# Segment sums of a Mamba scan taken as differences of running sums, in a fused Mamba and mixture-of-experts block

## The chip, the cores and the metric

The kernel runs on one core of a Trainium2 chip. The metric is the device time of one launch in microseconds (us). Engines are named as in the profile: PE is TensorE, PEld its weight loads, DVE is VectorE, ACT is ScalarE, POOL is GpSimd, SP issues the DMAs.

## The reference, cut to what matters

Eight sequences of 512 tokens with 128 channels go through two branches, which are multiplied: a Mamba-2 layer with an MLP, and a gated causal attention (16 heads of 8) followed by four dense experts.

```
zxbcdt = x @ in_proj_w.T
dt = softplus(zxbcdt[..., -4:] + dt_bias)           # 4 heads
A = -exp(A_log)
h = h * exp(dt_t * A) + (dt_t * x_t) outer B_t      # scan over 512 tokens
y = h @ C_t
...
s = x1 + mlp(layernorm(x1)),  x1 = xn + out_proj(rms(y * silu(z)))
g = silu(x2 + moe(rms(x2))),  x2 = xn + attention(rms(xn))
out = x + s * g
```

The scan is computed in four chunks of 128 tokens. Inside a chunk, output t takes input s with the weight exp(sum of dt*A over the tokens s+1 to t), for s <= t and for each of four heads. These sums, a 128 x 512 block per chunk (source token by head and target token), are the segment sums that the change is about.

## The kernel before, in words

One instruction stream per engine is written out by hand, with semaphores (`wait_ge`) between them. The engines go through rounds. Round r runs `stage_b` (the tail of sequence r: projections, experts, MLP; interleaved with the head of sequence r+1: input projections, convolution, attention score maxima) and then `stage_a` (attention and scan of sequence r+1). There is one head-only start (r = -1), a loop of seven full rounds, and one tail-only end. So `stage_a` runs eight times.

`stage_a` has 24 score units e, six (u = 0 to 5) for each of four head groups g. The scan's chunk g is dealt with in the same group. For the order around the change:

- PE: `exp_scores_of_four` (two units at once, from u = 0, 2, 4) waits for both exponentials of the pair before (`p_sb`). Behind it, at u = 0, come `weigh_values(e-2)`, `turn_y(g-1)` (transposes of the gated output), and `segments(g)`; at u = 2 `weigh_values`, `turn_values(g-1)`, `scan_inputs(g)`; at u = 4 `weigh_values`, `scan_outputs(g)`, and `new_state(g)` or, in the last group, `prep_a` (transposes of the next sequence's input).
- ACT: `exponentiate(e)` for each unit; between them `evac_values(g-1)` behind e = 6g, `evac_y(g-1)` behind e = 6g+1, and the exponential of the segment sums (into `es`) at u = 3 (u = 2 in group 0).
- POOL: the causal select of each unit (L1723, `pm_sb`), which `weigh_values` waits for; `xw` for the state; `decays(r, c)`, which multiplies a triangle of ones by dt*A of a chunk for four heads into `rs` (L1707); and small steps of the next input norm (`first_norms`, at e = 11, 13, 17).
- DVE: score maxima, `scan_products`, `scan_weights`, `scan_combine` (three operations behind `scan_outputs`), `scan_state` (the state update that frees PSUM bank R[1] for the next `segments`), the final gate and join.

Segment sums before: `segments(c)` is one fp32 matmul of `after` (ones where s > t) by `rs`, 128 x 512, into R[1]. The profile shows one fp32 matmul as two MATMUL records.

At the end of a round PE does `turn_y(3)`, `weigh_values(22)`, and then in `stage_b` the output projection `op` (L706), the transposes of the last attention values (L713), and the qkv projection of the next sequence. ACT does `evac_y(3)`, `square_y(3)`, `evac_values(3)`.

`cumulate` forms the running sums of dt*A (16 columns), the sums behind each token, and the totals, from which ACT takes `dec` (L1125).

Of the kernel before, what the change touches and what calls it, by code (L numbers as in the profile page):

```python
# [30 lines left out]
F32R = mybir.dt.float32r  # L31
# [13 lines left out]
G = 4  # L45
# [48 lines left out]
def build(nc, x, weights, vectors, rows, consts, out):  # L94
    with ExitStack() as ctx:
# [83 lines left out]
        rs = sb("rs", [P, 2, NH, P])  # L179
        es = sb("es", [P, 2, NH, P])  # L180
        gm = sb("gm", [P, 2, P])
# [30 lines left out]
        h2a = rs[:].rearrange("p k h t -> p k (h t)")  # L212
        h2b = es[:].rearrange("p k h t -> p k (h t)")
        h1a = wm[:].rearrange("p k h t -> p k (h t)")
        h1 = sb("h1", [P, 2, L])
        h3a = sb("h3a", [P, L])
# [56 lines left out]
        cum_ps = signal("cum_ps", 1)  # L273
        seg_ps = signal("seg_ps", T)
# [31 lines left out]
        dec_sb = signal("dec_sb", 1)  # L306
        seg_sb = signal("seg_sb", T)
# [29 lines left out]
        sv_sb = signal("sv_sb", 1)  # L337
        moe_sb = signal("moe_sb", T * E)
# [19 lines left out]
        rs_sb = signal("rs_sb", T)  # L358
# [84 lines left out]
        def _(pe):  # L443
# [253 lines left out]
            def stage_b(r, tail, head):  # L697
# [3 lines left out]
                if tail:  # L701

                    pe.wait_ge(yT_sb, at(yT_sb, r, 0))
# [5 lines left out]

                    pe.wait_ge(oT_sb, at(oT_sb, r, 0))  # L710
                    pe.wait_ge(yz_sb, at(yz_sb, r, 0))
                    for t in range(T):
                        i = pe.transpose(R[3][:, t * P:(t + 1) * P], oT[:, 1, t * P:(t + 1) * P], ident)  # L713
                    i.then_inc(ot3_ps, 1)
# [127 lines left out]
                if head:  # L842
                    exp_scores(r, 0)
# [12 lines left out]
            def stage_a(r):  # L856
                scan_inputs(r, 0)
                for e in range(G * UNITS):
# [34 lines left out]
                weigh_values(r, G * UNITS - 2)  # L893
# [7 lines left out]
            pe.wait_ge(pool_set, 10)  # L901
            pe.wait_ge(dve_set, 7)
# [14 lines left out]
        def _(act):  # L917
# [201 lines left out]
            def stage_a(r, tail):  # L1119
# [37 lines left out]
            act.wait_ge(pool_set, 3)  # L1157
            act.preload_act_table_set(EXP_LN)
# [17 lines left out]
        def _(dve):  # L1176
# [145 lines left out]
            def stage_b(r, tail, head):  # L1322
# [91 lines left out]
                if tail:  # L1414
                    for n in range(2):
# [7 lines left out]
                       ALU.add).then_inc(sv_sb, 1)  # L1423
                for t in range(T):
# [11 lines left out]
                    if head and t < 2:  # L1436
                        maxima(r, MAX_AT[t])

# [114 lines left out]
            dve.tensor_copy(maskb[:], future).then_inc(dve_set, 1)  # L1553
            ts(wqk[:], row[:, R_QN:R_QN + HD].unsqueeze(1).broadcast_to([P, AH, HD]), HD ** -0.5, None,
               ALU.mult).then_inc(dve_set, 1)
            dve.wait_ge(dve_set, 3)
# [7 lines left out]
            dve.wait_ge(dve_set, 7)  # L1564
# [21 lines left out]
        def _(pool):  # L1586
# [79 lines left out]
            def time_steps(r):  # L1666
# [29 lines left out]
                pool.sem_inc(pool_passed, 1)  # L1696
                pool.wait_ge(rs_sb, at(rs_sb, r, 0))
# [3 lines left out]
            def decays(r, c, tail):  # L1701

                pool.wait_ge(dt_sb, at(dt_sb, r, DT_STEPS))
                if c == 0 and tail:
                    pool.wait_ge(up_ps, at(up_ps, r, 9))
                pool.wait_ge(seg_ps, at(seg_ps, r, c - 1))
# [123 lines left out]
```

## Time and profile before

| | us |
|---|---|
| median of 3 runs | 869.19 (869.1 to 870.39) |
| profiled execution | 868.79 |
| its span, first to last instruction | 867.1 |
| PE busy | 786.9 |
| DVE busy | 618.0 |
| ACT busy | 499.2 |
| POOL busy | 323.9 |
| mean granted clock of PE | 0.992 of full speed |

1.7 us of the execution's time lies outside the span. A busy share says how long an engine had work in it, not that it set the time: in most stretches two or three engines wait for one another in turn, and what counts is which wait ends last.

### The profile page before, as it was taken

How to read it: one execution, taken by the hardware profiler on the slowest of the kernel's cores; microseconds unless marked ns; L12 is line 12 of the kernel's file. 1: busy time of each engine (PE TensorE's matmuls, PEld its weight loads, DVE VectorE, ACT ScalarE, POOL GpSimd, SP SyncE). 2: the span in 40 equal slices, each digit the busy share in tenths (PEclk: the TensorE clock that was granted, in tenths of full speed). 3: DMA queues.
4: the chain of work that ended last, by engine and by line, in shares of the span. 5: the costliest groups of instructions: out<-in, count | busy, mean ns of one | idle time of the engine just before them, and what ended most of it. 6: DMA issues, size and time to landing. Idle time of an engine off the chain costs nothing. (4 is left out here: it accounts for less than half of the span.)

```text
span 867.1 us, 18101 instructions
## 1 busy us (share of the span) xinstructions
PE 786.9 (91%) x5472; PEld 481.4 (56%) x5472; DVE 618.0 (71%) x1469; ACT 499.2 (58%) x928; POOL 323.9 (37%) x600
## 2 busy tenths in 40 slices
PE   2779999998999989998999989999899998999897
PEld 1455554755556564654647555474556556474555
DVE  2776479775888768776696768877587876967634
ACT  2335784466754775457744667537765568446552
POOL 5424533153512717045340545227160362505400
PEclk9998999999999999999999999999999999999999
DMA  4000000000000000000000000000000000000000
GB/s 165 2 8 20 8 0 2 9 15 25 0 8 12 14 12 0 8 14 24 0 0 8 14 24 0 2 18 2 24 0 8 13 25 0 0 8 14 24 2 13
DMA packets 15145, 11.73 MB, mean 14 GB/s; under 512 B 1040, under 2 KB 13968, under 8 KB 14992
## 3 DMA queue, kind: packets, MB, share of 16 engines
q1 hardware_dynamic: 15120, 11.43, 4.4%
q8 instruction: 12, 0.20, 0.1%
q14 instruction: 13, 0.11, 0.0%
HBM read 7.76 MB, written 2.10 MB: 11 GB/s over the span
## 5 line engine op out<-in xcount | busy, mean ns | idle before, releaser
L1102 ACT ACTIVATE sb_pr<-S 128x768 f32<-128x768 f32 (+1 forms) x192 | 163.8, 879 | 135.6 <-PE S L445 135.6
L1199 DVE TENSOR_REDUCE sb_mx<-S 128x2 f32<-128x256 f32 (+3 forms) x256 | 197.7, 816 | 29.3 <-PE S L445 28.8
L1723 POOL TENSOR_SCALAR_AFFINE_SELECT sb_pr<-sb_pr 128x256 f32<-128x256 f32 (+1 forms) x192 | 99.4, 523 | 299.3 <-ACT sb_pr L1102 299.0
L445 PE MATMUL R<-sb_pr,sb_va 128*32 128x512 f32 (+3 forms) x1024 | 89.4, 444 | 9.7 <-POOL sb_pr L1723 7.6
L445 PE MATMUL R<-sb_W,sb_pr 128*128 128x96 f32 (+1 forms) x512 | 69.5, 276 | 0.0
L445 PE MATMUL R<-sb_xfT,sb_W 128*128 128x512 f32 x144 | 69.2, 602 | 0.0
L445 PE MATMUL S<-sb_kT,sb_qT 32*128 32x256 f32 (+3 forms) x512 | 56.3, 384 | 13.8 <-DVE sb_mx L1199 10.9
L1187 DVE RECIPROCAL sb_rden<-R 128x16 f32<-128x16 f32 x32 | 8.2, 258 | 83.9 <-PE R L563 53.4
L445 PEld LDWEIGHTS R<-sb_W,sb_pr 128*128 128x128 f32 x512 | 63.5, 192 | 3.8 <-issue 3.5
L445 PEld LDWEIGHTS S<-sb_kT,sb_qT 32*128 32x128 f32 x512 | 27.5, 183 | 66.4 <-DVE sb_mx L1199 58.7
L445 PE MATMUL S<-sb_qT,sb_kT 32*128 32x256 f32 (+3 forms) x512 | 56.3, 384 | 2.9 <-ACT sb_pr L1102 1.9
L445 PEld LDWEIGHTS S<-sb_qT,sb_kT 32*128 32x128 f32 x512 | 27.3, 183 | 53.5 <-ACT sb_pr L1102 33.6
L1433 DVE SCALAR_TENSOR_TENSOR sb_x<-R,sb_wts,sb_x 128x96 f32<-128x96 f32 x128 | 40.6, 317 | 22.8 <-PE R L445 19.5
L445 PE MATMUL S<-sb_maskb,sb_identb 128*128 128x128 bf16 (+1 forms) x384 | 49.4, 241 | 0.0
L445 PEld LDWEIGHTS R<-sb_pr,sb_va 128*32 128x32 f32 x1024 | 23.5, 108 | 34.9 <-POOL sb_pr L1723 20.2
L965 ACT ACTIVATE sb_pr<-R 128x512 f32<-128x512 f32 x32 | 19.1, 598 | 39.1 <-PE R L445 39.0
L445 PE MATMUL R<-sb_rs,sb_cst 128*128 128x512 f32 x64 | 35.8, 642 | 5.7 <-DVE sb_x L1433 2.9
L1707 POOL TENSOR_TENSOR sb_rs<-sb_cst,sb_dta 128x512 f32<-128x512 f32 x32 | 40.5, 1265 | 1.2 <-POOL sb_dta L1698 1.1
L1626 POOL TENSOR_TENSOR sb_qk<-sb_qk,sb_wqk 128x512 f32<-128x512 f32 x8 | 10.1, 1269 | 81.9 <-ACT sb_sq L1000 81.9
L450 PE MATMUL S<-sb_cst,sb_tokqk 128*128 128x128 f32 x256 | 32.7, 285 | 4.5 <-DVE sb_tokqk L1385 2.2
L445 PEld LDWEIGHTS S<-sb_maskb,sb_identb 128*128 128x128 bf16 x384 | 23.8, 97 | 21.2 <-issue 17.5
L1217 DVE SCALAR_TENSOR_TENSOR sb_cv<-sb_xc,sb_vec,sb_cv 128x512 f32<-128x512 f32 x48 | 35.2, 734 | 0.0
(217 smaller groups left out, 1709.0 us busy)
## 6 DMA issues: line engine op xcount, KB each, us to landing
sb_xin<-x SPq DMA_DIRECT2D x9, 256.0 KB, 2.9
sb_W<-weights SPq DMA_DIRECT2D x1, 2290.0 KB, 10.9
sb_qT<-sb_mT SPq DMA_DIRECT2D x128, 4.0 KB
sb_xres<-x SPq DMA_DIRECT2D x8, 256.0 KB, 2.8
out<-sb_xres SPq DMA_DIRECT2D x7, 256.0 KB, 2.3
sb_cT<-sb_xact SPq DMA_DIRECT2D x8, 128.0 KB, 2.3
sb_W<-weights SPq DMA_DIRECT2D x1, 514.0 KB, 5.8
sb_cst<-consts SPq DMA_DIRECT2D x1, 328.0 KB, 3.1
```

The costliest lines, as they stand in the source:

```text
L445: return pe.matmul(o, lhsT, rhs, start=start, stop=stop, skip_group_check=True)
L450: i = pe.transpose(o[:, t * P:(t + 1) * P], src(t), ident)
L965: act.activation(dst, R[k % 4][:, :], func, bias=bias).then_inc(act_up, 1)
L1102: act.activation(pr[:, e % 4, :, 0:n], S[pair_of_exp(e)][:, :, 0:n], ACT.Exp).then_inc(p_sb, 1)
L1187: dve.reciprocal(rden[:], view[:, :, :, HD]).then_inc(done, 1)
L1199: o = dve.tensor_reduce(mx[:, n // P - 1, g, heads[0]:heads[1] + 1], found[:, :, at_col:at_col + n], AX.X, ALU.max, negate=True)
L1217: stt(out=cv[:, n], in0=xc[:, n, k:k + L], scalar=vcol(V_CONVW + TAPS * n + k), in1=cv[:, n], op0=ALU.mult, op1=ALU.add).then_inc(conv_dve, 1)
L1433: stt(out=x2[:, t, MASKED:D], in0=R[(22 + t) % 4][:, e * OC:(e + 1) * OC], scalar=wts[:, t, e:e + 1], in1=x2[:, t, MASKED:D], op0=ALU.mult ...
L1626: tt(qk[:, :, 0].rearrange("p t h d -> p t (h d)"), qk[:, :, 0].rearrange("p t h d -> p t (h d)"), wqk[:].rearrange("p h d -> p (h d)").un ...
L1707: tt(rs[:, c % 2], upto.unsqueeze(1).broadcast_to([P, NH, P]), dta[:, c, :].unsqueeze(2).broadcast_to([P, NH, P]), ALU.mult).then_inc(rs_s ...
L1723: pool.affine_select(out=keep, in_=keep, compare_op=ALU.is_ge, fill=0.0, base=0, pattern=pattern, channel_multiplier=-1)\
```

## The change

The running sums of dt*A, which `cumulate` already leaves in PSUM, are taken as cs[t], and a segment sum is cs[t] - cs[s]. So that fp32r operands carry enough digits, each sum is split into a rounded part and the rest. `sums_in_parts` (DVE, two operations of 128 x 32 elements) writes the parts of all four chunks and heads, `turn_sums` (PE) turns them with one 128 x 128 transpose, ACT makes from it `seg_v` and four left operands `seg_l`, and POOL one right operand `seg_r`, once per round. `segments(c)` is then one fp32r matmul of `seg_l[c]` by `seg_r` and one bf16 matmul that adds the large negative mask. `decays` goes. ACT makes its five operands right behind `exponentiate(0)`. Moves: on ACT `evac_values(g-1)` goes behind e = 6g+1, and at the end ahead of `evac_y(3)`; on PE `weigh_values(22)` goes ahead of `turn_y(3)`, the L713 transposes ahead of `op`, and `prep_a` ahead of `scan_outputs(3)`. The hidden layer `h2a` gets a tensor of its own, and there are a few more operations in the set-up.

```diff
+            def turn_sums(r):
+                pe.wait_ge(cs_sb, at(cs_sb, r, 2))
+                pe.wait_ge(act_up, at(act_up, r, 17))
+                pe.transpose(R[1][:, 0:P], cs[:].rearrange("p c k -> p (c k)"), ident).then_inc(csT_ps, 1)
+
             def segments(r, c):
 
-                pe.wait_ge(rs_sb, at(rs_sb, r, c + 1))
+                pe.wait_ge(segl_sb, at(segl_sb, r, 1 + T))
+                pe.wait_ge(segr_sb, at(segr_sb, r, 1))
...
-                mm(R[1][:, :], after, rs[:, c % 2].rearrange("p h t -> p (h t)")).then_inc(seg_ps, 1)
+                mm(R[1][:, :], seg_l[:, c, :], seg_r[:].rearrange("p h t -> p (h t)"), True, False)
+                mm(R[1][:, :].rearrange("p (h t) -> p h t", h=NH), maskb[:],
+                   identb[:].unsqueeze(1).broadcast_to([P, NH, P]), False, True).then_inc(seg_ps, 1)
...
# PE, experts_down
+                if t == 3 and head:
+                    pe.wait_ge(segl_sb, at(segl_sb, r, 1 + T))
...
# PE, stage_b: the L713 transposes now stand ahead of op; behind experts_down(r, 0, head):
+                    turn_sums(r)
                     exp_scores(r, 0)
...
# PE, stage_a
-                        scan_outputs(r, g)
                         if g == T - 1:
                             prep_a(r)
-                        elif g > 0:
+                        scan_outputs(r, g)
+                        if 0 < g < T - 1:
                             new_state(r, g)
...
+                weigh_values(r, G * UNITS - 2)
                 turn_y(r, T - 1)
-                weigh_values(r, G * UNITS - 2)
...
# ACT, stage_a
                     exponentiate(r, e)
-                    if u == 0 and g > 0:
+                    if e == 0:
+                        act.wait_ge(csT_ps, at(csT_ps, r, 1))
+                        act.wait_ge(segr_sb, at(segr_sb, r, 0))
+                        act.activation(seg_v[:], R[1][:, 0:P], ACT.Identity, bias=seg_sums[:, 1:2],
+                                       scale=seg_sums[:, 0:1]).then_inc(segl_sb, 1)
+                        act.wait_ge(seg_ps, at(seg_ps, r, 0))
+                        for c in range(T):
+                            act.activation(seg_l[:, c, :], R[1][:, 0:P], ACT.Identity, bias=seg_low[:, c:c + 1],
+                                           scale=seg_high[:, c:c + 1]).then_inc(segl_sb, 1)
+                    if u == 1 and g > 0:
                         evac_values(r, g - 1)
-                    if u == 1 and g > 0:
                         evac_y(r, g - 1)
...
+                evac_values(r, G - 1)
                 evac_y(r, T - 1)
                 square_y(r, T - 1)
-                evac_values(r, G - 1)
...
# DVE, stage_b, ahead of the experts' sums
+                if head:
+                    sums_in_parts(r)
...
+            def sums_in_parts(r):
+
+                total = S[0][:, 0, 0:T * NH].rearrange("p (c h) -> p c h", h=NH).unsqueeze(2)\
+                    .broadcast_to([P, T, 2, NH])
+                parts = cs[:, :, 0:16].rearrange("p c (x y h) -> p c x y h", x=2, y=2)
+                dve.wait_ge(dec_sb, at(dec_sb, r, 1))
+                dve.wait_ge(csT_ps, at(csT_ps, r, 0))
+                dve.tensor_copy(parts[:, :, :, 0].bitcast(F32R), total).then_inc(cs_sb, 1)
+                dve.wait_ge(cs_sb, at(cs_sb, r, 1))
+                tt(parts[:, :, :, 1], total, parts[:, :, :, 0], ALU.subtract).then_inc(cs_sb, 1)
...
# POOL
-            def decays(r, c, tail):
...
             def stage_a(r, tail):
-                decays(r, 0, tail)
+                pool.wait_ge(segl_sb, at(segl_sb, r, 1))
+                pool.sem_inc(pool_passed, 1)
+                pool.wait_ge(seg_ps, at(seg_ps, r, 0))
+                tt(seg_r[:], seg_v[:].unsqueeze(1).broadcast_to([P, NH, P]),
+                   seg_head[:].unsqueeze(2).broadcast_to([P, NH, P]), ALU.mult).then_inc(segr_sb, 1)
...
-                    if u == 3 and g < T - 1:
-                        decays(r, g + 1, tail)
```

## Rows read from the trace of the kernel before

**Rows 1.** The page, part 1: busy time of PE.
```profile
PE 786.9 (91%) x5472; PEld 481.4 (56%) x5472; DVE 618.0 (71%) x1469; ACT 499.2 (58%) x928; POOL 323.9 (37%) x600
```

**Rows 2.** Timeline (start, length, instruction, idle): ACT, once a round.
```profile
260.46 0.21 ACT L1125 ACTIVATE sb_dec<-S 128x48 f32<-128x48 f32 x1 [3.27 <-PE S L445]
...
362.07 0.21 ACT L1125 ACTIVATE sb_dec<-S 128x48 f32<-128x48 f32 x1 [3.28 <-PE S L445]
...
465.01 0.21 ACT L1125 ACTIVATE sb_dec<-S 128x48 f32<-128x48 f32 x1 [3.27 <-PE S L445]
```

**Rows 3.** Timeline from 287.5 to 291.3: how group 2 begins.
```profile
287.59 0.51 PE L445 MATMUL S<-sb_qT,sb_kT 32*128 32x512 f32 x4
...
288.03 0.86 PE L445 MATMUL R<-sb_pr,sb_va 128*32 128x256 f32 x16
...
288.83 0.42 DVE L1511 TENSOR_TENSOR sb_hst<-R,sb_hdec 64x256 f32<-64x256 f32 x1
289.07 0.59 ACT L942 ACTIVATE sb_oT<-R 128x512 f32<-128x512 f32 x1
...
289.30 1.12 PE L445 MATMUL R<-sb_rs,sb_cst 128*128 128x512 f32 x2
...
289.55 1.03 ACT L1102 ACTIVATE sb_pr<-S 128x1024 f32<-128x1024 f32 x1
...
290.63 0.19 PEld L445 LDWEIGHTS S<-sb_qT,sb_kT 32*128 32x128 f32 x4 [1.03 <-ACT sb_pr L1102]
```

**Rows 4.** Groups by line and form, all engines: busy, mean ns of one.
```profile
L445 PE MATMUL S<-sb_maskb,sb_identb 128*128 128x256 bf16 x128 | 20.9, 276 | 0.0
L926 ACT ACTIVATE sb_va<-S,sb_ratio 128x128 f32<-128x128 f32 x32 | 11.5, 360 | 0.0
```

**Rows 5.** Timeline from 280 to 281.7: how group 1 begins.
```profile
280.12 1.02 PE L445 MATMUL R<-sb_rs,sb_cst 128*128 128x512 f32 x2
280.15 1.03 ACT L1102 ACTIVATE sb_pr<-S 128x1024 f32<-128x1024 f32 x1
...
281.23 0.19 PEld L445 LDWEIGHTS S<-sb_qT,sb_kT 32*128 32x128 f32 x4 [0.91 <-ACT sb_pr L1102]
```

**Rows 6.** Timeline from 294.5 to 301.7: how group 3 begins.
```profile
294.53 1.49 POOL L1707 TENSOR_TENSOR sb_rs<-sb_cst,sb_dta 128x512 f32<-128x512 f32 x1
...
295.04 1.52 DVE L1452 TENSOR_TENSOR sb_gs<-sb_x,sb_gs 128x512 f32<-128x512 f32 x1
...
298.15 0.86 PE L445 MATMUL R<-sb_pr,sb_va 128*32 128x256 f32 x16 [0.66 <-POOL sb_pr L1723]
...
299.69 1.12 PE L445 MATMUL R<-sb_rs,sb_cst 128*128 128x512 f32 x2 [0.31 <-DVE sb_hst L1511]
...
301.62 1.07 PE L445 MATMUL R<-sb_pr,sb_va 128*32 128x512 f32 x8 [0.42 <-POOL sb_pr L1723]
```

**Rows 7.** Timeline from 253 to 267.2: score masks; ACT and PE behind the first unit.
```profile
253.79 0.61 PE L445 MATMUL S<-sb_maskb,sb_identb 128*128 128x256 bf16 x4
...
262.67 1.02 ACT L1102 ACTIVATE sb_pr<-S 128x1024 f32<-128x1024 f32 x1 [2.00 <-PE S L445]
...
265.14 1.02 ACT L1102 ACTIVATE sb_pr<-S 128x1024 f32<-128x1024 f32 x1 [1.44 <-PE S L445]
...
267.18 0.61 PE L445 MATMUL R<-sb_W,sb_pr 128*128 128x96 f32 x4
```

**Rows 8.** Timeline from 306.6 to 312: the end of a round on PE.
```profile
308.33 0.44 PE L627 MATMUL R<-sb_cst,sb_yz 128*128 128x128 f32 x2 [0.99 <-DVE sb_yz L1499]
308.70 0.86 PE L445 MATMUL R<-sb_pr,sb_va 128*32 128x256 f32 x16
...
311.81 2.75 PE L445 MATMUL S<-sb_W,sb_xbT 128*128 128x384 f32 x8
```

**Rows 9.** Windows of 2 us from 426: busy by engine, then the granted clock.
```profile
428.00:430.00 2.00, 2.00 (x12) 2.00 (x11) 0.99 (x2) 1.15 (x4) 2.00 (x3) 0.50 0.00 0
```

**Rows 10.** Timeline: the last tail's value transposes on PE, and what waits.
```profile
822.00 0.66 PE L450 MATMUL R<-sb_cst,sb_ao 128*128 128x128 f32 x4 [0.68 <-DVE sb_ao L1189]
```

More of the change, by code:

```diff
@@ L178, in build @@
         dec = sb("dec", [P, 3, T, NH])
-        rs = sb("rs", [P, 2, NH, P])
         es = sb("es", [P, 2, NH, P])
+        cs = sb("cs", [P, T, 32])
+        seg_v = sb("seg_v", [P, P])
+        seg_l = sb("seg_l", [P, T, P], F32R)
+        seg_r = sb("seg_r", [P, NH, P], F32R)
+        seg_low = sb("seg_low", [P, T])
+        seg_high = sb("seg_high", [P, T])
+        seg_sums = sb("seg_sums", [P, 2])
+        seg_head = sb("seg_head", [P, NH])
         gm = sb("gm", [P, 2, P])
@@ L215, in build @@
         h1 = sb("h1", [P, 2, L])
+        h2a = sb("h2a", [P, 2, L])
         h3a = sb("h3a", [P, L])
@@ L273, in build @@
         cum_ps = signal("cum_ps", 1)
+        csT_ps = signal("csT_ps", 1)
         seg_ps = signal("seg_ps", T)
@@ L306, in build @@
         dec_sb = signal("dec_sb", 1)
+        segl_sb = signal("segl_sb", 1 + T)
         seg_sb = signal("seg_sb", T)
@@ L337, in build @@
         sv_sb = signal("sv_sb", 1)
+        cs_sb = signal("cs_sb", 2)
         moe_sb = signal("moe_sb", T * E)
@@ L701, in stage_b @@
                 if tail:
+                    pe.wait_ge(oT_sb, at(oT_sb, r, 0))
+                    pe.wait_ge(yz_sb, at(yz_sb, r, 0))
+                    for t in range(T):
+                        i = pe.transpose(R[3][:, t * P:(t + 1) * P], oT[:, 1, t * P:(t + 1) * P], ident)
+                    i.then_inc(ot3_ps, 1)
                     pe.wait_ge(yT_sb, at(yT_sb, r, 0))
@@ L708, in stage_b @@
                     i.then_inc(op_ps, 1)
[L710 to L714, printed above, removed]
                 if head:
@@ L900, in _ @@
             pe.wait_ge(c_loaded, 48)
-            pe.wait_ge(pool_set, 10)
-            pe.wait_ge(dve_set, 7)
+            pe.wait_ge(pool_set, 11)
+            pe.wait_ge(dve_set, 13)
             pe.wait_ge(xab_sb, at(xab_sb, -2, 1))
@@ L1157, in _ @@
             act.wait_ge(pool_set, 3)
+            act.wait_ge(dve_set, 6)
             act.preload_act_table_set(EXP_LN)
@@ L1553, in _ @@
             dve.tensor_copy(maskb[:], future).then_inc(dve_set, 1)
+            by_part = ident.rearrange("p (c k) -> p c k", c=T)
+            dve.tensor_reduce(seg_low[:], by_part[:, :, 0:8], AX.X, ALU.add).then_inc(dve_set, 1)
+            dve.tensor_reduce(seg_high[:], by_part[:, :, 8:16], AX.X, ALU.add, negate=True).then_inc(dve_set, 1)
+            dve.wait_ge(dve_set, 4)
+            dve.tensor_reduce(seg_sums[:, 0:1], seg_low[:], AX.X, ALU.add).then_inc(dve_set, 1)
+            dve.tensor_reduce(seg_sums[:, 1:2], seg_high[:], AX.X, ALU.add, negate=True).then_inc(dve_set, 1)
+            dve.tensor_reduce(sp[:, 0], by_part[:, :, 0:16].rearrange("p c (m h) -> p c h m", h=NH),
+                              AX.X, ALU.add).then_inc(dve_set, 1)
+            dve.wait_ge(dve_set, 7)
+            dve.tensor_reduce(seg_head[:], sp[:, 0].rearrange("p c h -> p h c"), AX.X,
+                              ALU.add).then_inc(dve_set, 1)
             ts(wqk[:], row[:, R_QN:R_QN + HD].unsqueeze(1).broadcast_to([P, AH, HD]), HD ** -0.5, None,
                ALU.mult).then_inc(dve_set, 1)
-            dve.wait_ge(dve_set, 3)
+            dve.wait_ge(dve_set, 9)
             tt(wqk[:], wqk[:], row[:, R_KN:R_KN + HD].unsqueeze(1).broadcast_to([P, AH, HD]),
@@ L1695, in time_steps @@
                 pool.wait_ge(cum_ps, at(cum_ps, r, 0))
-                pool.sem_inc(pool_passed, 1)
-                pool.wait_ge(rs_sb, at(rs_sb, r, 0))
                 tt(dta[:], dt[:], neg_a[:].unsqueeze(1).broadcast_to([P, T, NH]),
                    ALU.mult).then_inc(dt_sb, 1)
-            def decays(r, c, tail):
[L1703 to L1706, printed above, removed]
-                tt(rs[:, c % 2], upto.unsqueeze(1).broadcast_to([P, NH, P]),
-                   dta[:, c, :].unsqueeze(2).broadcast_to([P, NH, P]), ALU.mult).then_inc(rs_sb, 1)
-            def stage_a(r, tail):
-                decays(r, 0, tail)
+            def stage_a(r, tail):
+                pool.wait_ge(segl_sb, at(segl_sb, r, 1))
[3 more added lines that the diff above has]
+                   seg_head[:].unsqueeze(2).broadcast_to([P, NH, P]), ALU.mult).then_inc(segr_sb, 1)
                 for e in range(G * UNITS):
@@ L1748, in _ @@
             pool.memset(xc[:, :, 0:3], 0.0).then_inc(pool_set, 1)
+            pool.memset(cs[:], 0.0).then_inc(pool_set, 1)
             pool.memset(cT[:], 0.0).then_inc(pool_set, 1)
```

7 lines of the change are left out of this document (3 added, 4 removed).

## The prediction

> **What bounds the kernel now.** I read the page first. PE is busy for 91% of the span [rows 1], so it looks like the bound; but the change takes work from PE and POOL and gives some to ACT, and whether that pays is decided wait by wait. Next the round: ACT's `dec` comes at 260.46 and 362.07 [rows 2], so a full round lasts 101.61 us. `stage_a` runs eight times, and its rounds look alike.
>
> Then the timeline of one `stage_a`, around each `segments(g)`. In the middle of a group (u = 2 to 5) PE goes from one matmul into the next, and everything else is early. At its beginning it is not PE that decides. In group 2 the scores start at 287.59, the segment matmul runs from 289.30 to 290.42, and PE then waits: the next scores start at 290.63, behind ACT [rows 3]. ACT is held by `evac_values`, which stands between the two exponentials: it starts at 289.07, and the second exponential at 289.55. Group 1 is the same: segment matmul 280.12 to 281.14, scores at 281.23 [rows 5]. In group 3 two more waits appear: `weigh_values(16)` waits for POOL's select until 298.15, and `weigh_values(18)` until 301.62 [rows 6]. POOL had `decays(3)` from 294.53 to 296.02 ahead of these selects. The reader is to see three waits in these rows: ACT's order, POOL's queue, and the state update of DVE that lets each segment matmul begin.
>
> **The segment pass.** Out goes an fp32 matmul of 1.02 to 1.12 us [rows 3, 5]; in come an fp32r and a bf16 one of 512 columns. The trace has no fp32r matmul over 128 rows. The nearest row is the scores': four of 32 rows and 512 columns side by side in 0.51 us [rows 3], with the next instruction 0.44 behind their start. The bf16 mask of 256 columns takes 276 ns, and four of them 0.61 us [rows 4, 7], so each further one 0.11 and 512 columns 0.22. Together some 0.75 us until PE is free, 0.3 to 0.35 less than now. The bounds: half of that fp32r price, if the four row strips shared a rate that one matmul has alone (0.22 less), and the whole fp32 price (0.85 for the stream, so the pair is 0.2 slower than now). I take 0.44, since that is a measured spacing.
>
> The Trainium skill ("FP8 and Floating Point Precision", TensorE Precision Notes) says that true FP32 takes four passes through the array and reduced-precision FP32 is read and truncated; one of four passes of a 0.85 us stream would be 0.21 us, and the forecast some 2.5 us lower. The scores' 0.44 us [rows 3] doesn't show that price.
>
> **Group 1.** ACT now runs both exponentials in a row. The second would start 0.48 earlier (the 289.07 and 289.55 of [rows 3]), at 279.67, and end at 280.70 [rows 5]. The new segment pair frees PE at 280.12 + 0.75 = 280.87. So the scores go at 280.85 instead of 281.23: gain 0.38. What is late next is PE itself. `evac_values` and `evac_y` now come behind the exponential, in time the scores need anyway.
>
> **Group 2.** It starts 0.38 early. The state update of DVE ends at 289.25 before [rows 3], now 288.87; the segment pair frees PE at 289.67; the second exponential ends at 290.58 - 0.38 - 0.48 = 289.72. Scores at 289.77 against 290.63: 0.86 early in all, so 0.48 more. The select that `weigh_values` needs follows the exponential, thus moves with it.
>
> **Group 3.** It starts 0.86 early. The decays are gone from POOL, so selects 16 and 17 are done before PE asks, and the 0.66 wait [rows 6] goes. What is late next is the scan on DVE: the segment matmul waits for its state update (0.31 in the row) and starts at 299.69 [rows 6]. Ahead of it stands L1452, which took 1.52 us while POOL worked in the same time [rows 6]; without `decays` I give it 0.2 (the bounds: nothing and 0.6). So the segment pair starts 0.86 + 0.2 early, at 298.63, and is done at 299.45 (0.8 with its end) against 299.69 + 1.12 = 300.81: 1.35 early. Then `weigh_values(18)` no longer waits 0.42 [rows 6] for a select behind POOL's norm steps: 1.77 early.
>
> **Group 0.** The segment matmul gets shorter between waits for DVE's maxima; I cost it at nothing. Of the four shortened matmuls none pays by PE's work alone.
>
> **The end of the round.** `prep_a` (four transposes, 0.66 with their end [rows 10], so some 0.5 of PE) now stands ahead of `scan_outputs(3)`, and `weigh_values(22)` (0.86 [rows 8], 0.78 without its end) fills the wait for DVE, of which 0.99 is in the row of `turn_y(3)` [rows 8]. Moving 0.5 out of that hole and 0.78 into it, and a wait of 0.1 for `yT` behind the L713 transposes, leaves 0.2 gain, to the qkv projection at 311.81 [rows 8]. `prep_a` waits for DVE's norms and the last `seg_sb`; both are over 1 us early.
>
> **What is added.** `turn_sums` is one transpose, a quarter of four in 0.66 [rows 10], so some 0.15 us on PE, between `experts_down(0)` and the first scores; I count it in full. DVE's two small operations lie in its wait for the experts. The five ACT reads are the largest addition: 128 x 128 from PSUM takes 0.36 [rows 4], so 1.8 us behind the first exponential, 263.69 to 265.5. The second exponential stood at 265.14 [rows 7], so it comes 0.3 late, but PE asks for it only behind `experts_down(3)`. `experts_down(3)`, now waiting for `seg_l`, stands at 267.10 to 267.18 [rows 7]: 1.6 us of cover. At twice the price per read it would be gone, at 0.2 a round. POOL's one product (1.49 at most, as `decays` in [rows 6]) is queued ahead of the first select, whose result PE wants behind the experts and `segments(0)`, over 5 us later.
>
> **The sum.** Per round 0.38 + 0.48 + 0.91 + 0.2 - 0.15, = 1.82; eight times, 14.6 us. The head-only start loses some 1.15: there the sums, the transpose and ACT's reads have no experts to lie behind (0.7 and 0.3), and a memset is ahead of the first norm on POOL (0.15). The last tail gains 0.8: the value transposes come ahead of `op`, which covers the DVE step for which PE waited 0.68 [rows 10]. Net -14.3 on the profiled execution's 868.8 (867.1 span and 1.7 around it): 854.5. That execution is 0.4 below the median shown, so against the median 854.9.
>
> **The rivals.**
> - *Only POOL's queue pays.* ACT does the same work in another order, and if the next exponential is held by the displaced evacuations, the 0.38 and 0.48 are given back. For it: 0.59 of `evac_values` [rows 3] and the evacuation of y now stand together ahead of it. Against it: PE waits for the exponential before, not for this one. Left are 0.91 + 0.2 - 0.15 = 1 us a round: 861. The same time comes about when the fp32r pass costs like the fp32 one: then PE is free only 1.2 us behind each start, and groups 1 and 3 lose 0.4 each, some 862. Chance 0.17 together.
> - *Hidden anyway.* The shift made in `stage_a` is lost in `stage_b` to something that doesn't move with it, or the clock takes most of it: 867.5 to 871. Nothing in the rows is tied to a fixed time; the DMAs have microseconds of slack. Chance 0.04.
> - *Slower: the clock.* In one round, at 428 to 430, the granted clock stood at 0.50 [rows 9], the lower level of 1.2 GHz, after a sparse stretch of PE around the small projections, where it did not fall in the other rounds. That round took 102.94 us against 101.61 [rows 2]: one such dip costs 1.3 us. The change makes PE idler and shifts the rounds. One dip in every round would take back 6 x 1.3 = 8 us; from two in a round, 2.6 against the 1.8 gained, it decides: some 874. Against it: the waits that go are PE's, so busy share hardly falls. The Trainium skill ("TensorE: Matmul & The Clock Gate", What's actually happening) says that the throttled state is the default and activity releases it; by that rule an idler PE is at risk, and the row of the dip agrees with it. Chance 0.09.
> - *The forecast*, all three group starts pay: 0.70.
>
> **How the numbers follow.** Predicted 854.9. Cheap fp32r (-2.5), the 0.6 on L1452 (-2.8) and a cheaper end (-1.5) reach to 848; the first rival reaches to 862, and with a dip in some rounds 863. The range is 848 to 863; below it 0.08 is left and above it 0.12. Within 0.2% (1.7 us, about what a measurement can tell from no change): 0.04. Faster: 0.87. Slower: 0.09.
>
> **What the profile after would show.** Segment pairs of about 0.8 us. In groups 1 and 2, scores right behind the second exponential, about 0.4 and 0.9 us earlier in the round, `weigh_values(16)` without a wait for POOL, and 1.8 us gained by the qkv projection. POOL some 30 us less busy, ACT some 10 to 15 more. A round of 99.8 us. It would be wrong if ACT's reads took twice 0.36, if `experts_down(3)` or `prep_a` showed a wait, or if the clock were at 0.5 in stretches where it is now full.

## The result, and the profile after

| | before | after |
|---|---|---|
| median | 870.85 us (869.1 to 873.39, 20 runs) | 866.61 us (861.57 to 868.76, 20 runs) |
| ratio | | 0.9940, 95% interval 0.9925 to 0.9954 |
| profiled execution | 868.79 | 867.78 |
| its span | 867.1 | 865.9 |
| mean granted clock of PE | 0.992 | 0.973 |

The change gains 0.6%, 4 us; 854.9 was forecast, and the time lies outside the range of 848 to 863. The runs of after spread over 7.2 us where those of before spread over 4.3, and the time goes with the clock: the runs of 861.57 to 862.08 us show a mean of 0.983, those of 867.5 to 868.8 us 0.972 to 0.974.

The page, part 1 (busy time, share, instructions), of the kernel after, against [rows 1]:
```profile
PE 786.7 (91%) x5480; PEld 490.6 (57%) x5480; DVE 615.6 (71%) x1491; ACT 511.0 (59%) x968; POOL 296.0 (34%) x577
```
POOL lost 27.9 us and ACT gained 11.8, as expected. PE's busy time fell by 0.2 us only, although its work shrank: at a lower clock the same work is busy for longer, and the mean clock fell from 0.992 to 0.973. That is the first hint.

ACT's `dec` in the timeline of after, against [rows 2]:
```profile
262.46 0.21 ACT L1146 ACTIVATE sb_dec<-S 128x48 f32<-128x48 f32 x1 [3.28 <-PE S L455]
...
362.23 0.21 ACT L1146 ACTIVATE sb_dec<-S 128x48 f32<-128x48 f32 x1 [3.27 <-PE S L455]
...
464.79 0.21 ACT L1146 ACTIVATE sb_dec<-S 128x48 f32<-128x48 f32 x1 [3.28 <-PE S L455]
```
One round takes 99.77 us, 1.83 less than 101.60 and what was forecast (1.82). The next takes 102.56. The eight `dec` of an execution bound seven intervals: the first is the round behind the start, the other six are called the full rounds here:

| us | 1st (start) | full rounds 2 to 7 |
|---|---|---|
| before | 96.72 | 101.59, 101.61, 102.94, 101.60, 101.59, 101.60 |
| after | 97.83 | 101.23, 99.77, 102.56, 102.57, 102.60, 101.15 |

After has three lengths: 99.8, 101.2 and 102.6. In what follows a place is given by its distance behind the `dec` of its round, and a low stretch is one at a granted clock of 0.50. Windows of 2 us of after, 10 us behind the `dec` of 362.23 (PE, PEld, DVE, ACT and POOL busy, granted clock, DMA share, GB/s):
```profile
372.00:374.00 2.00, 1.10 (x5) 0.47 (x4) 1.93 (x6) 1.48 (x3) 0.99 (x2) 1.00 0.00 0
374.00:376.00 2.00, 1.96 (x12) 0.45 (x12) 1.85 (x4) 1.08 (x2) 0.41 (x1) 0.77 0.00 0
376.00:378.00 2.00, 2.00 (x18) 1.70 (x15) 0.81 (x2) 0.81 (x1) 0.17 (x1) 0.50 0.00 0
378.00:380.00 2.00, 2.00 (x21) 1.65 (x20) 1.37 (x6) 0.35 (x1) 0.47 (x1) 0.88 0.00 0
```
The same two windows of before:
```profile
372.00:374.00 2.00, 1.58 (x6) 0.60 (x6) 1.76 (x5) 1.08 (x3) 0.99 (x2) 1.00 0.00 0
374.00:376.00 2.00, 2.00 (x20) 0.87 (x20) 1.87 (x3) 1.36 (x4) 1.03 (x2) 1.00 0.00 0
```
In after PE's clock falls to its lower level, 1.2 GHz, behind a stretch in which PE was busy for 1.10 of 2 us; before it was busy for 1.58 there, and the clock held. Read over the whole trace, the full rounds of after hold eight such low stretches: five some 12 us behind `dec`, in group 0, of which one is shown, and three some 63 us behind it, around the small projections, where before had its only one [rows 9]. Rounds with none take 99.77, with one 101.15 or 101.23, with two 102.56 to 102.60: each costs 1.4 us. Six rounds took 609.88 us, and 6 x 99.77 would be 598.6: the low stretches cost 11.3 us of this execution. It took 867.78 us, 13.3 more than the 854.5 forecast for it.

A sparse place alone doesn't make the clock fall. This is the round of after that has no low stretch (262.46), and the disturbed one (362.23), each from 10 us behind its `dec`:
```profile
272.46:274.46 2.00, 1.25 (x6) 0.64 (x6) 1.93 (x6) 1.48 (x3) 0.99 (x2) 1.00 0.00 0
372.23:374.23 2.00, 1.26 (x6) 0.65 (x6) 1.93 (x6) 1.48 (x3) 0.99 (x2) 1.00 0.00 0
```
PE is as idle in the one as in the other, and the clock fell behind the second only. Before has 1.64 to 1.65 in these 2 us of every full round. So the change made the place sparser in all six rounds, and the clock fell there in five.

The timeline of PE in group 0 of before, same round:
```profile
372.29 1.10 PE L445 MATMUL R<-sb_rs,sb_cst 128*128 128x512 f32 x2 [0.41 <-DVE sb_x L1433]
373.32 0.44 PE L445 MATMUL S<-sb_qT,sb_kT 32*128 32x384 f32 x2
373.88 0.44 PE L445 MATMUL S<-sb_kT,sb_qT 32*128 32x384 f32 x2
```
and of after:
```profile
372.44 0.47 PE L455 MATMUL R<-sb_seg_r,sb_seg_l 128*128 128x512 f32 x1 [0.41 <-DVE sb_x L1465]
...
372.75 0.39 PE L455 MATMUL R<-sb_identb,sb_maskb 128*128 128x512 bf16 x1
...
373.07 0.44 PE L455 MATMUL S<-sb_qT,sb_kT 32*128 32x384 f32 x2
...
374.04 0.44 PE L455 MATMUL S<-sb_kT,sb_qT 32*128 32x384 f32 x2 [0.53 <-DVE sb_mx L1229]
```
Less `dec` (362.07 and 362.23), the second half of the scores goes at 11.81 in both. The shorter segment sum gained nothing up to there; it became 0.53 us of waiting for DVE, next to a wait of 0.41 that was there already. The prediction costed group 0 at nothing, nearly rightly as work. The wait that came of it is where the clock now falls.

The other place, around the small projections, is a different matter. PE in it, before (behind the `dec` of 260.46):
```profile
319.69 0.66 PE L450 MATMUL R<-sb_cst,sb_x1n 128*128 128x128 f32 x4 [0.92 <-DVE sb_x1n L1355]
...
321.97 0.66 PE L450 MATMUL R<-sb_cst,sb_xf 128*128 128x128 f32 x4 [0.32 <-DVE sb_xf L1369]
...
323.40 1.05 PE L445 MATMUL R<-sb_W,sb_xfT 128*128 128x4 f32 x8 [0.34 <-ACT sb_xfT L1032]
```
and after (262.46):
```profile
319.84 0.66 PE L460 MATMUL R<-sb_cst,sb_x1n 128*128 128x128 f32 x4 [0.93 <-DVE sb_x1n L1385]
...
322.12 0.66 PE L460 MATMUL R<-sb_cst,sb_xf 128*128 128x128 f32 x4 [0.33 <-DVE sb_xf L1399]
...
323.56 1.05 PE L455 MATMUL R<-sb_W,sb_xfT 128*128 128x4 f32 x8 [0.34 <-ACT sb_xfT L1053]
```
The waits are the same within 0.01 us. That this place has three low stretches where it had one is thus not because work was taken from it.

Groups 1 to 3 are nearly as foreseen. Group 2 in the undisturbed round, against [rows 3]:
```profile
289.58 1.94 ACT L1123 ACTIVATE sb_pr<-S 128x1024 f32<-128x1024 f32 x2 [1.86 <-PE S L455]
...
290.25 0.42 DVE L1554 TENSOR_TENSOR sb_hst<-R,sb_hdec 64x256 f32<-64x256 f32 x1
...
290.73 0.49 PE L455 MATMUL R<-sb_seg_r,sb_seg_l 128*128 128x512 f32 x1
...
291.06 0.10 PEld L455 LDWEIGHTS R<-sb_identb,sb_maskb 128*128 128x128 bf16 x1
291.06 0.39 PE L455 MATMUL R<-sb_identb,sb_maskb 128*128 128x512 bf16 x1
291.40 0.60 ACT L963 ACTIVATE sb_oT<-R 128x512 f32<-128x512 f32 x1
291.57 0.19 PEld L455 LDWEIGHTS S<-sb_qT,sb_kT 32*128 32x128 f32 x4 [0.41 <-ACT sb_pr L1123]
```
The next matmul goes 0.33 us behind the start of the fp32r pass. The two exponentials stand together (x2, from 289.58), and `evac_values` starts at 291.40, behind both. Scores go at 291.57, 29.11 behind `dec`; before at 30.17 (290.63 - 260.46).

Group 3, against [rows 6]:
```profile
295.99 1.12 DVE L1495 TENSOR_TENSOR sb_gs<-sb_x,sb_gs 128x512 f32<-128x512 f32 x1
...
297.57 2.07 POOL L1666 TENSOR_TENSOR sb_lnv<-sb_lnv,sb_minus_half 128x8 f32<-128x8 f32 x1
...
298.37 0.86 PE L455 MATMUL R<-sb_pr,sb_va 128*32 128x256 f32 x16
...
300.32 0.47 PE L455 MATMUL R<-sb_seg_r,sb_seg_l 128*128 128x512 f32 x1 [0.43 <-DVE sb_hst L1554]
...
302.02 1.07 PE L455 MATMUL R<-sb_pr,sb_va 128*32 128x512 f32 x8 [0.61 <-POOL sb_pr L1770]
```
`weigh_values(16)` (at 298.37) no longer waits. DVE's step (L1495, L1452 before) takes 1.12 where it took 1.52, the 0.4 within its bounds. But `weigh_values(18)` (at 302.02) still waits for POOL, 0.61, behind the norm steps (2.07 for one of them): the prediction's step that said this wait goes was wrong.

### The profile page after: what moved, and what is told of

It reads as the page before. It is cut to its first block and busy times, and to the rows that moved or that the text cites. A ratio compares the mean times of both kernels' runs of the same rounds, so it can differ in the third digit from the quotient of the medians.

```text
span 865.9 us, 18165 instructions
## 1 busy us (share of the span) xinstructions
PE 786.7 (91%) x5480; PEld 490.6 (57%) x5480; DVE 615.6 (71%) x1491; ACT 511.0 (59%) x968; POOL 296.0 (34%) x577
## 5 line engine op out<-in xcount | busy, mean ns | idle before, releaser
L1123 ACT ACTIVATE sb_pr<-S 128x768 f32<-128x768 f32 (+1 forms) x192 | 161.7, 883 | 127.0 <-PE S L455 127.0
L455 PE MATMUL R<-sb_pr,sb_va 128*32 128x512 f32 (+3 forms) x1024 | 93.4, 460 | 6.6 <-POOL sb_pr L1770 4.3
L455 PE MATMUL S<-sb_kT,sb_qT 32*128 32x256 f32 (+3 forms) x512 | 58.3, 393 | 17.0 <-DVE sb_mx L1229 14.7
L1757 POOL TENSOR_TENSOR sb_seg_r<-sb_seg_v,sb_seg_head 128x512 fp32r<-128x512 f32 x8 | 8.3, 1042 | 174.9 <-ACT sb_seg_v L1154 174.9
L455 PE MATMUL S<-sb_qT,sb_kT 32*128 32x256 f32 (+3 forms) x512 | 58.3, 393 | 1.7 <-ACT sb_pr L1123 0.8
L460 PE MATMUL S<-sb_cst,sb_tokqk 128*128 128x128 f32 x256 | 38.7, 321 | 3.5 <-DVE sb_tokqk L1415 2.2
L460 PEld LDWEIGHTS S<-sb_cst,sb_tokqk 128*128 128x128 f32 x256 | 36.1, 169 | 5.2 <-DVE sb_tokqk L1415 2.6
L1680 POOL TENSOR_TENSOR sb_qk<-sb_qk,sb_wqk 128x512 f32<-128x512 f32 x8 | 10.2, 1270 | 79.8 <-ACT sb_sq L1021 79.8
```

What stands on the lines that cost most here:

```text
L455: return pe.matmul(o, lhsT, rhs, start=start, stop=stop, skip_group_check=True)
L460: i = pe.transpose(o[:, t * P:(t + 1) * P], src(t), ident)
L1123: act.activation(pr[:, e % 4, :, 0:n], S[pair_of_exp(e)][:, :, 0:n], ACT.Exp).then_inc(p_sb, 1)
L1680: tt(qk[:, :, 0].rearrange("p t h d -> p t (h d)"), qk[:, :, 0].rearrange("p t h d -> p t (h d)"), wqk[:].rearrange("p h d -> p (h d)").un ...
L1757: tt(seg_r[:], seg_v[:].unsqueeze(1).broadcast_to([P, NH, P]), seg_head[:].unsqueeze(2).broadcast_to([P, NH, P]), ALU.mult).then_inc(segr_ ...
```

## The experiments

Three theories stood. **A**: work was taken from PE where it waits anyway, PE gets idler there, and its clock falls. **B**: the low stretches hang on the length of the round and on when its places come, not on the work in them. **C**: the added work costs more than was reckoned. A "filler" is the kernel's own `dense`: fp32 matmuls of 256 columns whose result nobody reads. Ratios are against the kernel before on the same chip, with 95% intervals. Counts of low stretches are of each kernel's one traced execution.

**Fillers in group 0 (e1), around the small projections (e2), in both (e3).** To the kernel after:
```diff
# e1, PE, stage_a, at e = 3, and ahead of segments(r, 0)
+    dense(R[3][:, 0:256], 1)
# e2, PE, stage_b: ahead of the transposes of x1n (2) and xf (1), and of the gate's matmuls (1)
+    if head:
+        dense(R[1][:, 0:256], 2)
```


> The changed kernel with two more fp32 matmuls of 256 columns per round on PE, whose results nobody reads, in the two waits of group 0: one between the masks of unit 2 and segments(0), one between exp_scores(3) and max_scores. Theory A (the work that the change takes away lets PE's clock fall): the stretches at a granted clock of 0.5 in group 0 of the full rounds (five in the profile of the changed kernel) go, those in stage_b stay, and the time falls by 5 to 7 us to about 860. Theory B (the clock falls by the round's length and phase, wherever PE stands): as many stretches as before, elsewhere, 866. Theory C (what is lost is the added work of ACT and PE, not the clock): 866 to 868, with the matmuls on top.

> The changed kernel with four more such matmuls per round in stage_b, in the waits ahead of the x1n transposes (two), the xf transposes (one) and the gate (one). Theory A: the stretches at 0.5 in stage_b (four in the profile of the changed kernel) go, those in group 0 stay; the time falls by 4 to 5 us to about 862. Theory B: no fewer stretches, 866 to 868. Theory C: 866 to 868.

> Both sets of added matmuls. Theory A: a full round takes 99.8 to 100.2 us every time, with no stretch at 0.5 in the seven full rounds; 854 to 857. Theory B: 865 or more. Theory C: 866 to 869.

Measured: e1 864.15 us (0.9909, 0.9883 to 0.9935), e2 858.97 (0.9865, 0.9849 to 0.9881), e3 859.07 (0.9855, 0.9836 to 0.9873). Theory A had said 860, 862 and 854 to 857: e2 is faster than that, e1 and e3 are slower, and e1's interval overlaps that of after (0.9925 to 0.9954). In the full rounds of e1 no low stretch was left at 12 us; behind the start, the tail included, there are four at 60 to 63 and three new ones at 39. Its traced execution, at 870.13 us, is the slowest of its six; it is at the lower clock for 17.1 us behind the first `dec`, and its second `dec` comes 3.1 later than that of after. In e2 those at 63 are gone from the full rounds, and two remain there at 12. In the full rounds of e3 two remain, both at 39. The place of the new ones, in windows of e1 (columns as above):
```profile
403.00:405.00 2.00, 1.50 (x8) 0.16 (x8) 0.52 (x2) 1.93 (x3) 1.26 (x4) 0.72 0.45 131
405.00:407.00 2.00, 2.00 (x13) 1.89 (x9) 0.55 (x2) 0.00 (x0) 0.01 (x1) 0.50 0.45 124
```
That is the part of group 3 in which PE waits for DVE's state update and POOL's select. Added work made the kernel faster in e2 and e3, which C can't give, and each place that was filled lost its low stretches in the full rounds, for A. But a place that was quiet in after took some over, and in e2 the clock fell at 12 in two rounds of six, although PE was as idle there as in after (1.24 to 1.26 us of 2) in all six: in which round, and at which of several sparse places, the clock falls is not fixed by the place alone, and so much of B stands.

**The moves alone (e4).** The kernel before, with the moves on ACT and PE and the old segment sums:
```diff
-                    if u == 0 and g > 0:
+                    if u == 1 and g > 0:
                         evac_values(r, g - 1)
...
-                turn_y(r, T - 1)
                 weigh_values(r, G * UNITS - 2)
+                turn_y(r, T - 1)
```


> The kernel before with the moves alone: evac_values behind the second exponential and ahead of evac_y(3), weigh_values(22) ahead of turn_y(3), the L713 transposes ahead of op, prep_a ahead of scan_outputs(3); segment sums as before, with decays on POOL. By my steps the moves give 0.2 in groups 1 and 2 (PE is then held by the 1.1 us segment matmul, not by ACT), nothing in group 3 (POOL's queue stays), 0.2 at the end and 0.8 in the last tail: 0.5 a round, 5 us, 865 to 866. If the moves alone carry the gain: 859 or less. If they give nothing without the shorter pass: 869 to 870. The clock should stay at full speed in group 0, as the fp32 matmul stands there.

Measured 860.09 us (0.9872, 0.9858 to 0.9887): 6.5 us faster than the whole change, and 5 faster than expected. Full rounds take 100.53 us, 1.07 less than before, none with a low stretch. The expectation gave 0.5 a round, since PE would be held by the long segment matmul. By the places of `weigh_values` behind `dec` the moves alone give 0.35 in group 1 and 0.47 in group 2, nearly all of the forecast's 0.38 and 0.48, nothing in group 3, and 0.25 at the end of the round. So these two steps need ACT's order only, not the shorter pass.

**The segment sums alone (e6).** The kernel after with every move undone.

> The changed kernel's segment sums alone: every move (the evacuations on ACT, the last weighing, the turned values and the turned input on PE) is undone. The moves alone gave 1.07 us a round against the kernel before and brought no low stretch in full rounds. Theory A: undisturbed rounds of 100.8 to 101.2 us (0.4 to 0.8 under the 101.60 of before), with low stretches at about 12 us behind dec, since the shorter passes of group 0 are here, perhaps at 64 too; then 868 to 873, no faster than the kernel before. Theory B (phase of the round): no fixed place. Theory C (the low stretches need the moves and the segment sums together): none in full rounds and 863 to 866.

Measured 870.95 us (1.0011, 0.9990 to 1.0033): no gain. Undisturbed rounds take 100.89, 0.71 less than before, which over six rounds is 4.3 us; but three of the six have a low stretch, two at 40 us and one at 12, at 1.4 to 1.6 us each. Of the 0.71, 0.14 comes in group 0 and 0.56 in group 3, nothing in groups 1 and 2. The two halves are worth 1.07 and 0.71 a round, 1.78 against the 1.83 together: they add up. Theory A gave the time and the round's length, but it had put the low stretches at 12.

**The first segment sum in full fp32 (e5).** The work in one place changes, and nothing is added whose result isn't used. To the kernel after:
```diff
-                mm(R[1][:, :], seg_l[:, c, :], seg_r[:].rearrange("p h t -> p (h t)"), True, False)
+                left, right = seg_l[:, c, :], seg_r[:].rearrange("p h t -> p (h t)")
+                if c == 0:
+                    left, right = left.bitcast(F32), right.bitcast(F32)
+                mm(R[1][:, :], left, right, True, False)
```


> The changed kernel, but the first of the four segment sums of a round is taken in full fp32 (the same operands, read as fp32); nothing else moves. The pass then takes about 1.0 us where it took 0.5, in group 0 alone, where PE waits for DVE anyway (0.41 and 0.53 us). Theory A (a PE whose work was taken away lets its clock fall): the low stretches some 12 us behind dec go, as they did when filling matmuls were put in that place; those 63 us behind dec in the small projections stay, perhaps with one at 39. Rounds without a low stretch 99.8 us, time 860 to 866. Theory B (the low stretches follow from the length and the phase of the round, not from the work in the place): as many low stretches as in the changed kernel, 866 to 868. Theory C (the full fp32 pass costs its own time): rounds without a low stretch 100.3 us.

Measured 859.45 us (0.9854, 0.9834 to 0.9875), 7 us faster than after, with one pass a round made slower. Timeline of PE in e5, 10 us behind its `dec` of 361.08:
```profile
371.30 1.10 PE L455 MATMUL R<-sb_seg_r,sb_seg_l 128*128 128x512 f32 x2 [0.42 <-DVE sb_x L1468]
372.23 0.38 PE L455 MATMUL R<-sb_identb,sb_maskb 128*128 128x512 bf16 x1
372.54 0.44 PE L455 MATMUL S<-sb_qT,sb_kT 32*128 32x384 f32 x2
372.90 0.44 PE L455 MATMUL S<-sb_kT,sb_qT 32*128 32x384 f32 x2
```
The second scores go at 11.82, as in after (11.81), now without a wait. PE is busy for 1.77 to 1.78 of the 2 us from 10 us behind `dec`. No low stretch stands at 12, and only one in all full rounds, at 39. The rounds without one take 100.08, 0.31 more than 99.77: C's price for it. That the low stretches at 63 went too, where nothing was changed, is more than A had said, and speaks for the part of B that stands.

**Every sparse place filled (e7).** The places of e1 and e2, two in group 3 and five fillers in the head-only start:
```diff
+                    if not tail:
+                        dense(R[0][:, 0:256], 2)
                     turn_sums(r)
                     exp_scores(r, 0)
...
+                        if g == 3:
+                            dense(R[3][:, 0:256], 1)
                         segments(r, g)
```


> The changed kernel with matmuls of 256 columns, whose results nobody reads, in every wait of PE near which a low stretch was seen: two in group 0, four around the small projections, two in group 3, and five in the head-only start. Theory A: no low stretch in the full rounds, each 99.8 us; the low stretch of 10 to 14 us in the start is shorter; 853 to 856, near the forecast of 854.9. Rival (the fillers cost what they cover, or the low stretches appear in another place, as the one at 39 us did when group 0 alone was filled): 858 to 861.

Measured 854.27 us (853.81 to 855.23; 0.9809, 0.9796 to 0.9823), the fastest of all kernels here and 0.6 from the forecast. The page, part 1, of e7:
```profile
PE 798.4 (94%) x5610; PEld 499.4 (59%) x5610; DVE 614.3 (72%) x1491; ACT 510.1 (60%) x968; POOL 297.0 (35%) x577
```
Timeline of PE in its group 0:
```profile
367.87 0.65 PE L455 MATMUL R<-sb_cst 128*128 128x256 f32 x2
368.45 0.47 PE L455 MATMUL R<-sb_seg_r,sb_seg_l 128*128 128x512 f32 x1
...
369.45 0.70 PE L455 MATMUL R<-sb_cst 128*128 128x256 f32 x2
370.08 0.44 PE L455 MATMUL S<-sb_kT,sb_qT 32*128 32x384 f32 x2
```
PE does 12 us more and the kernel ends 12 us sooner. Six full rounds take 99.74 to 99.80 us, the clock is at 0.999, and the one low stretch stands at the very end. The fillers lie in the waits and cost the round nothing (99.77 in the undisturbed round of after). Against after, the profiled spans differ by 13.8: 11.3 in the six rounds, 2.6 ahead of the second `dec`.

**Control: fillers where PE had no wait (e8).** To the kernel after, in group 1 at u = 4:
```diff
+                        if g == 1:
+                            pe.wait_ge(gm_sb, at(gm_sb, r, g + 1))
+                            dense(R[2][:, 0:256], 2)
```


> Control: the changed kernel with two such matmuls a round at a place where PE has no wait (group 1, ahead of the last part of the group). Theory A: the low stretches at 12 and 63 us behind dec stay as in the changed kernel, since nothing is filled there, and the rounds are up to 0.9 us longer: 867 to 874. Theory B (any change of the round's length shifts the low stretches away): fewer of them, 860 to 865.

Measured 876.00 us (1.0067, 1.0043 to 1.0092). This is 2 us above the range of A. The full rounds hold eight low stretches, five of them at 12, two at 42 and one at 66. A longer round with more work on PE doesn't help in itself, which speaks against B as the whole cause. The rounds' own cost was more than expected: the one without a low stretch took 101.33, 1.56 above 99.77, where up to 0.9 was said. Timeline of PE in that round:
```profile
183.72 1.13 PE L455 MATMUL R<-sb_cst 128*128 128x256 f32 x4 [0.47 <-DVE sb_gm L1519]
184.78 0.85 PE L455 MATMUL R<-sb_pr,sb_va 128*32 128x384 f32 x8
```
The two fillers take 1.06, and the `wait_ge` that was put ahead of them holds PE for 0.47 more. So the control adds a short wait as well as work; no low stretch stands near it (24 us).

Over the 14 traced kernels PE is busy for 1.24 to 1.26 us of the 2 from 10 us behind `dec` in four (after, e2, e6, e8), and in 13 of their 24 full rounds the clock fell there. In the other ten it is busy for 1.64 or more, and in their 60 full rounds the clock never fell there.

**The same fillers in the kernel before (e9).**

> The kernel before, with the same filling matmuls as in e7_fill_all. This tells what the fillers are worth without the change. Theory A (the kernel before loses to the clock only one low stretch in its full rounds and part of the start, where e7 lost nothing more): full rounds stay at 101.60 us, without the one of 102.94; the start gains about 1 to 2 us; 866 to 868, ratio 0.995 to 0.998. Then the change itself, with the clock held in both, is worth 12 to 14 us. Rival (most of the 17 us that e7 gained over the kernel before come from the fillers, not from the change): 858 to 862.

Measured 873.12 us (1.0032, 1.0022 to 1.0043), worse than before. Both expectations had it faster than before. All full rounds take 102.00 to 102.03, without a low stretch, 0.4 more than 101.60. The second scores of group 0 go 12.25 us behind `dec`, 0.42 later than in before, and that is all that the round loses: before has no wait as long as the filler there (0.63 us). The first `dec` comes 3.2 us later too (65.39, not 62.15), and the second 4.1 later, most of the loss, although both kernels have 6.8 us at the lower clock ahead of it; what the fillers hold up in the start was not looked into. The fillers don't make a kernel faster as such; against this one, e7 is 18.9 us ahead.

**ACT's order undone (e10), PE's order at the end undone (e12), all sums in fp32 (e11), each in e7.** Here round lengths read prices. They ran on another chip than e7, so rounds without a low stretch are compared, not times; e10 and e12 still have two low stretches each in the full rounds, all four 48 us behind `dec`.
```diff
# e10: ACT, stage_a and its end, as before the change
-                    if u == 1 and g > 0:
+                    if u == 0 and g > 0:
                         evac_values(r, g - 1)
# e12: PE, the L713 transposes behind op, prep_a behind scan_outputs(3), weigh_values(22) last
-                weigh_values(r, G * UNITS - 2)
                 turn_y(r, T - 1)
+                weigh_values(r, G * UNITS - 2)
# e11
+                mm(R[1][:, :], seg_l[:, c, :].bitcast(F32), seg_r[:].bitcast(F32).rearrange(...), True, False)
```


> e7_fill_all, with ACT's order as in the kernel before: the evacuation of the values stands again between the two exponentials of a group's first pair, and last at the end of a round. The clock stays full, so the round length reads the price of that order alone. The prediction's steps for groups 1 and 2 (0.38 and 0.48): rounds of about 100.6 us, 861. Rival (only POOL's queue and the shorter passes pay, the next exponential doesn't decide): 99.8 us, 854.

> e7_fill_all, with PE's order as in the kernel before at the end of a round: the turned input behind the last scan outputs, the last weighing behind the turned y, the output projection ahead of the turned values. The prediction's step: 0.2 a round and 0.8 in the last tail, so rounds of about 99.97 us and 856.5. Rival (the end of the round was worth more than I gave it, since the moves alone gained 1.07 a round where ACT's order explains 0.5 to 0.9): rounds of 100.2 to 100.4 us, 858 to 860.

> e7_fill_all, with all four segment sums of a round in full fp32 (same operands, read as fp32). With the first one alone in fp32 a round took 100.08 us, 0.3 more than 99.77. The prediction's step: 0.4 lost in group 1 and 0.4 in group 3, none in group 2, so with the 0.3 of group 0 rounds of 100.9 us, 862. Rival (in groups 1 to 3 PE waits for something else behind the segment sum, so the shorter pass is worth nothing there): 100.1 us, 856.5.

Measured: e10 876.38 us (1.0069, 1.0055 to 1.0083), undisturbed rounds 101.90; e12 871.63 (1.0013, 1.0003 to 1.0023), 101.06; e11 867.77 (0.9974, 0.9963 to 0.9985), 101.45. All three cost more than any theory said. Set against e7 by the exponentials' times behind `dec`, e10 is 0.43 late at group 2's first exponential, 0.91 at group 3's and 0.90 at the last of group 3, where the forecast had 0.38 + 0.48. Then it loses 1.2 more at the end of the round. e12 loses nothing until there, and then 1.3. Timeline of e10 at the end of a round:
```profile
313.19 0.38 ACT L990 ACTIVATE sb_yT<-R 128x256 f32<-128x256 f32 x1 [1.79 <-PE R L645]
...
313.87 0.59 ACT L984 ACTIVATE sb_oT<-R 128x512 f32<-128x512 f32 x1
...
314.51 0.66 PE L726 MATMUL R<-sb_cst,sb_oT 128*128 128x128 f32 x4 [1.36 <-ACT sb_oT L984]
```
and of e12:
```profile
208.08 0.60 ACT L984 ACTIVATE sb_oT<-R 128x512 f32<-128x512 f32 x1 [0.89 <-PE R L455]
208.57 0.38 ACT L990 ACTIVATE sb_yT<-R 128x256 f32<-128x256 f32 x1
...
209.00 2.05 PE L455 MATMUL R<-sb_W,sb_yT 128*128 128x128 f32 x16 [0.99 <-ACT sb_yT L990]
```
PE asks for the values first and ACT gives y first, or the other way round: 1.36 and 0.99 us of waiting. Both in the old order (e6 undoes both) the end costs 0.26 more than both in the new one; 0.2 was forecast. At the end of the round the two orders are one edit; either half alone is 1.2 to 1.3 us a round slower than both, and 1 us slower than neither. e11 loses 0.61 in group 0 (0.31 in e5, where no filler stands beside it), 0.35 in group 1, 0.18 in group 2 and 0.56 in group 3. Its pair is a full fp32 pass and the mask, longer than the one matmul of before; against it, and in the order of after, the shorter pair pays in every group.

## Why the prediction was wrong

- **The undisturbed round: right, in part by luck.** 99.77 against 99.8. By its steps, behind `dec`: group 1's scores 0.63 early (0.38 said), group 2's 1.06 (0.86), `weigh_values(18)` 1.60 (1.77), the qkv projection 1.85 (1.97 before the 0.15 of `turn_sums`). Up to group 2 the steps gave 0.2 more than said, from there to `weigh_values(18)` 0.54 where 0.91 was said, and the errors cancel. The group 0 that was costed at nothing gave 0.14 of the first. `turn_sums` put the first exponential 0.19 late, and nothing of it was left 9.7 us behind `dec`: it had cover, and 0.15 was counted that wasn't paid. The 0.38 and 0.48 were put down to ACT's order and the shorter pass together; e4 shows nearly all of them with the long pass.
- **Group 3: half right.** The select wait at 16 went, DVE's L1452 took 0.40 less where 0.2 was taken, and the segment pair starts 1.37 early (1.06 said). The wait at 18 stayed, because POOL's own norm steps, not `decays`, hold it.
- **The segment pass: the pair was sized too high.** The next matmul comes 0.31 to 0.33 us behind the start of the fp32r one, against 0.44 taken and a lower bound of 0.22; the bf16 mask takes 0.32 where 0.22 was taken. In groups 0 and 3 the pair takes 0.63 to 0.64 where 0.75 was said. The forms, grouped (busy, mean ns | idle before):
```profile
L455 PE MATMUL R<-sb_seg_r,sb_seg_l 128*128 128x512 f32 x32 | 15.6, 488 | 6.5 <-DVE sb_hst L1554 3.0 <-DVE sb_x L1465 2.9
...
L455 PE MATMUL R<-sb_identb,sb_maskb 128*128 128x512 bf16 x32 | 12.7, 398 | 0.0
```
Full fp32 would not have cost 0.8 a round, as the first rival said: in e11 it cost 1.68, of which 0.61 in group 0, that the rival had at nothing.
- **ACT's reads: right.** From the first (265.78) to the end of the fifth 1.85 us, 1.8 said. The second exponential came 0.35 late (0.3 said), and `experts_down(3)` shows no wait.
- **The end of the round and the last tail: right.** 2.5 us from the last `dec` to the end of the span (97.3 to 94.8), against 1.8 + 0.8.
- **The start: too cheap.** The first `dec` is 1.25 late and the round behind it 1.11 longer, so the second `dec` is 2.4 late. By the forecast it would be 0.7 early, 1.15 lost and 1.82 gained: 3.0 us missed. This too goes with the clock. Ahead of the second `dec` before has 6.8 us at the lower level (64 to 72 us); after has 10.2 us there, and 3.4 more each at 30 and at 122 us. e7, with none at all ahead of its second `dec`, has it 0.2 earlier than before.
- **The clock: the step that failed.** "The waits that go are PE's, so busy share hardly falls", chance 0.09, and a term of nothing for it in the sum. It was named with its place at the small projections, its price (1.3, measured 1.4) and its sign, a clock at 0.5 where it was full; "two in a round" was given as the point from which it decides. What the sentence missed is that not all of the removed time was waiting, and that the other places were sparse already: at `segments(0)` PE's work went and a wait of the same size came. The busy share of the whole span says nothing of it (91% in both); in the 2 us from 10 us behind `dec` PE's busy time fell from 1.65 to 1.25. Of the 13.3 us that the profiled execution missed by, the eight low stretches are 11.3 and the start 3.0; 1.3 go the other way, the low stretch that before had in its own full rounds [rows 9]. That the time is lost to the clock is shown by the round lengths and by e7; that the low stretches at 12 need the idler group 0 is shown by e1, e5 and e7, with e8 as the control. Not shown is why the three at 63 came, in a place that the change left as it was, why they go when only group 0 changes (e5), and which sparse place falls next (39 us in e1, e3 and e5).
- **Its arithmetic.** The terms add up to -14.2, not -14.3. Two low stretches in each of six rounds would by its own prices give 854.9 + 15.6, some 870.5, not 874; neither changes the outcome.

The Trainium skill ("TensorE: Matmul & The Clock Gate", A second HAM failure mode: psum-queue depth-cycling) tells of a kernel whose PE idles briefly but often between groups of matmuls, so that its clock goes up and down. The trace agrees in so far as no wait of PE beside the low stretch at 12 us is longer than 0.53 us; here two such waits stand there, not many.

## What to carry to other kernels

Before taking work from PE, look at what stands behind it: where PE then waits for another engine, the time isn't gained, and the clock may be lost, as in group 0 here. Read the granted clock by windows, not the mean or the busy share, and compare the round that has no low stretch with those that have. If the clock is the loss, idle matmuls in exactly the waits can give it back (e7); where there was no wait, or a shorter one, they cost their own time (e8, e9). Where one engine feeds another in a given order, as at the end of the round here, price the change of both orders together.

## What was not expected of the hardware

- A slower instruction made the kernel faster: one fp32r pass of 512 columns a round turned back into fp32 (0.31 us a round) gained 7 us of 867 (e5).
- PE's clock falls in a kernel in which PE is 91% busy, behind two waits of 0.41 and 0.53 us, though not in every round that has them (five of six in after, two of six in e2); each fall costs 1.4 us.
- An fp32r matmul of 128 rows and 512 columns lets the next one go after 0.31 to 0.33 us, where fp32 took 0.93 (371.30 to 372.23 in e5) and bf16 0.31 to 0.32.
